# Gathering the rows of the first four expert blocks on chip, by matmuls with slot matrices

## The chip, the cores and the metric

The kernel runs on one core of one Trainium2 chip. The metric is device time of one execution in microseconds (us). A core has five engines that run their own instruction streams and meet at semaphores: TensorE (PE, matmuls and transposes into PSUM), VectorE (DVE), ScalarE (ACT), GpSimd (POOL, which here issues the indirect DMAs) and SyncE (SP, which here issues the plain DMAs). PEld is TensorE's loading of weights, which overlaps its matmuls.

## The reference

The kernel computes an audio tower for 64 samples of 10 tokens each (640 tokens of 128 features): a patch projection with a layer norm, one attention layer of 8 heads with a distance bias, and a mixture of 16 experts, of which each token uses the best two. The part that matters here is the last one:

```
router_logits = x @ router_w.T
top_vals, top_idx = jax.lax.top_k(router_logits, TOP_K)
weights = jax.nn.softmax(top_vals.astype(jnp.float32), axis=-1)
...
def step(acc, ew):
    wg, wu, wd, ce = ew
    hid = jax.nn.silu(x @ wg) * (x @ wu)
    y = hid @ wd
    return (acc + ce[:, None] * y, None)
```

The kernel computes an expert only for the tokens that chose it. All arithmetic is in float32.

## The kernel before

Tokens lie in five tiles t = 0..4 of 128 (one token per partition). After attention each tile goes through a chain of its own: PE projects it (`project(t)`), DVE and ACT normalise it into `pay[:, 0, t, 0:128]` (`normalised(t)`), PE transposes it (`normal_T(t)`) and multiplies it with the router (`logits(t)`), DVE takes the best two experts (`best(t)`, `route(t)`, which ends in `mask[:, t, :]`), PE counts with a triangular matrix how many tokens have gone to each expert so far (`ranks(t)`, `later_rows(t)`), and DVE reads out of these counts the slot of each token at each of its two experts (`place(t)`, which ends in `slot[:, t, :]`).

A slot is a row of `disp`, a buffer in memory of 16 x 640 rows; expert e owns the rows from 640 e on. A row has 131 numbers: 128 features and three that travel with them (where the result belongs, the weight, the token's number). POOL sends every tile twice, once for each choice: ten indirect DMAs (`dispatch(t, j)`, line 386). When all ten have landed (semaphore `s_disp`), SP loads the first 128 rows of experts 0, 1, 2, 3 into four buffers `xs` (line 327) and later, as buffers come free, those of the others (line 332).

An expert block e (there are 17: the 16 experts and one overflow block) then is: PE transposes its rows (`rows_T`, line 1082), ACT copies them to `xsT` and the three numbers to `meta` (`take_rows`, lines 556 and 557), PE multiplies with gate and up weights (`gate_up`, four matmuls, line 1087), ACT applies silu (line 562), DVE multiplies (`gated`, line 825), PE multiplies with the down weights (`down`, two matmuls, line 1095). A float32 matmul stands in the trace as two MATMUL instructions. PE runs its instructions in the written order: `rows_T(e+3)`, `gate_up(e+2)`, `down(e)`. For blocks 0 to 11 DVE scales the result (`result`, lines 831 and 832) and POOL sends it to `ybuf` in memory (line 395); SP fetches all of `ybuf` back (`yb`) once the twelve sends have landed. The last five blocks are added in PSUM by matmuls with 0/1 matrices that DVE makes (`spread`, `combine`, line 1103). Lines 877 to 883 add everything up on DVE.

Between the end of the routing and the first rows PE has nothing to do. The program fills part of this with matmuls of zeros (`keep_clock`, line 892), 24 of them from tile 3's ranks on, 16 of these behind the last `later_rows`.

When its counting is done, DVE runs a chain of small instructions that decide about overflow blocks (lines 797 to 819); the first `gated` stands behind it.

Of the kernel before, what the change touches and what calls it, by code (L numbers as in the profile page):

```python
# [10 lines left out]
ALU = mybir.AluOpType  # L11
# [3 lines left out]
P = 128  # L15
B = 64
S = 10
T = S // 2
D = 128
# [19 lines left out]
EARLY = 2  # L39

# [41 lines left out]
def audio_tower(nc, first, rows_d, gb, t_head, table, toks, expert_w, out):  # L82
    with ExitStack() as ctx:
# [78 lines left out]
        iota = sb("iota", [P, TOK])  # L162
        comb = sb("comb", [P, TAIL, TOK])
# [82 lines left out]
        comb_ready = sem("comb_ready")  # L246
        yt_ready = sem("yt_ready")
# [20 lines left out]
        GATE, ROWS_T, RESULT = (1, 3, 4, 0), 5, (7, 2)  # L268
        FIRST_ROWS = (5, 7, 2)
# [29 lines left out]
        OVER_ROWS = 4  # L299

        def combined(t):

            return ps[:, (6, 3)[t // 4], (t % 4) * D:(t % 4 + 1) * D]
# [4 lines left out]
        def _(sp):  # L308
# [17 lines left out]
            for u in range(NBUF):  # L326
                sp.dma_start(xs[:, u, :], disp[u * TOK:u * TOK + P, :]).then_inc(xs_in[u], 16)
            with sp.Fori(1, E // NBUF) as g:
                for u in range(NBUF):
                    row = sp.snap((g * NBUF + u) * TOK)  # L330
                    sp.wait_ge(xs_used, g * NBUF + (u - NBUF + 1))
                    sp.dma_start(xs[:, u, :], disp[bass.ds(row, P), :]).then_inc(xs_in[u], 16)
# [5 lines left out]
            sp.wait_ge(xs_used, E - NBUF + 1)  # L338
# [72 lines left out]
        def _(act):  # L411
# [141 lines left out]
            def take_rows(b, src, e, bank=ROWS_T):  # L553

                act.wait_ge(xsT_ps, e + 1)
# [8 lines left out]
            def take_result(b, n, e):  # L564

                act.wait_ge(y_ps, e + 1)
                nc.scalar.copy(yt[:, n, :], ps[:, RESULT[b], 0:D]).then_inc(yt_ready, 1)

            AHEAD = 3
            for e in range(AHEAD):  # L570
                take_rows(e, e, e, FIRST_ROWS[e])
            with act.Fori(0, E // NBUF - 1) as g:
                for u in range(NBUF):
                    silu(u, g * NBUF + u)
                    take_rows((u + AHEAD) % NBUF, (u + AHEAD) % NBUF, g * NBUF + (u + AHEAD))
            for e in range(E - NBUF, BLK):
# [18 lines left out]
        def _(dve):  # L595
# [150 lines left out]

            def place(t):
                dve.wait_ge(rank_ps, t + 1)
                need(mark(nc.vector.tensor_tensor(spick[:, t, :, :], oh[:, t, :, :],
                                                  count_ps().unsqueeze(1).broadcast_to([P, TOPK, E]), ALU.mult)))  # L750
                with nc.allow_low_precision(reason="one whole number below 2**24 among zeros"):
                    nc.vector.tensor_reduce(slot[:, t, :], spick[:, t, :, :], AX_X, ALU.add).then_inc(slot_ready, 1)

# [25 lines left out]
            route(1)  # L779
            stream_stats(3)  # L780
            place(1)
            best(2)
            normalised(3)
# [6 lines left out]
            place(3)  # L790
            best(4)
            route(4)
            place(4)

# [33 lines left out]
            def result(b, u, e):  # L828

                dve.wait_ge(y_ps, e + 1)  # L830
                nc.vector.tensor_copy(yi[:, u:u + 1], meta[:, bass.ds(e, 1), 0:1].rearrange("p a c -> p (a c)"))
                nc.vector.tensor_scalar(ys[:, u, :], ps[:, RESULT[b], 0:D],  # L832
                                        meta[:, bass.ds(e, 1), 1:2].rearrange("p a c -> p (a c)"), None,
                                        ALU.mult).then_inc(y_ready, 1)

            def spread(n, e):

                dve.wait_ge(xs_used, e + 1)
                dve.wait_ge(in_toks, 16)
                m = meta[:, bass.ds(e, 1), :].rearrange("p a c -> p (a c)")  # L840
                nc.vector.tensor_scalar(comb[:, n, :], iota[:, :], m[:, 2:3], m[:, 1:2],
                                        ALU.is_equal, ALU.mult).then_inc(comb_ready, 1)
# [12 lines left out]
            with dve.Fori(1, E // NBUF - 1) as g:  # L855
                for k in range(NBUF):
                    finish(k, g * NBUF + k)
                    gated((k + 2) % NBUF, g * NBUF + (k + 2))
            n_over = dve.value_load(ctl[0:1, 0:1], min_val=0, max_val=NOV)
            for e in range(E - NBUF, BLK):  # L860
# [25 lines left out]
        def _(pe):  # L886
# [176 lines left out]
            logits(3)  # L1063
            later_rows(2)
            keep_clock(2, FREED)
            ranks(3)
            normal_T(4)
            keep_clock(1, FREED)
            logits(4)
            later_rows(3)  # L1070
            keep_clock(3, FREED)
            ranks(4)
            keep_clock(2, FREED)
            later_rows(4).then_inc(cnt_ps, 1)
            keep_clock(16, FREED)
# [8 lines left out]
            def gate_up(b, e, w):  # L1084
                pe.wait_ge(xsT_ready, e + 1)
                for c in range(4):
                    last = mm(ps[:, GATE[b], c * P:(c + 1) * P],  # L1087
                              expW[:, w * WROW + c * P:w * WROW + (c + 1) * P], xsT[:, b, :], start=True, stop=True)
                last.then_inc(g_ps, 1)

            def down(b, r, e, w):
                pe.wait_ge(hid_ready, e + 2)
                for c in range(2):
                    a = w * WROW + 2 * F + c * D
                    last = mm(ps[:, RESULT[r], 0:D], hid[:, b, c, :], expW[:, a:a + D], start=(c == 0), stop=(c == 1))  # L1095
# [11 lines left out]
            def step(e):  # L1107

                if e + 3 < BLK:
                    n = (e + 3) % NBUF  # L1110
                    pe.wait_ge(xsT_ready, e + 3)
                    rows_T(n, e + 3, xs_in[n], 16 * ((e + 3) // NBUF + 1))
# [72 lines left out]
```

## Time and profile before

| | |
|---|---|
| time, median of 3 runs (lowest to highest) | 98.06 us (97.67 to 98.19) |
| profiled execution: its own time, its span | 97.58 us, 95.4 us |
| PE busy | 86.2 us, 90% of the span |
| DVE, ACT, POOL busy | 56.5 us (59%), 36.2 us (38%), 33.2 us (35%) |
| chain that ended last, by engine | PE 81%, DMA 4%, ACT 4%, issue 2%, DVE 2% |

The span runs from the first to the last instruction that the profiler recorded; 2.18 us of the profiled execution's time lie around it. The shares are averages over stages; what matters below is one stage, from about 47 us (the last tiles are routed) to about 63 us (the expert blocks run at their full pace). "Chain that ended last" follows the work back from the last instruction to what released it. PEclk is the clock that TensorE was granted, 1.00 being 2.4 GHz and 0.50 being 1.2 GHz.

### The profile page before, as it was taken

How to read it: one execution, taken by the hardware profiler on the slowest of the kernel's cores; microseconds unless marked ns; L12 is line 12 of the kernel's file. 1: busy time of each engine (PE TensorE's matmuls, PEld its weight loads, DVE VectorE, ACT ScalarE, POOL GpSimd, SP SyncE). 2: the span in 40 equal slices, each digit the busy share in tenths (PEclk: the TensorE clock that was granted, in tenths of full speed). 3: DMA queues.
4: the chain of work that ended last, by engine and by line, in shares of the span. 5: the costliest groups of instructions: out<-in, count | busy, mean ns of one | idle time of the engine just before them, and what ended most of it. 6: DMA issues, size and time to landing. Idle time of an engine off the chain costs nothing.

```text
span 95.4 us, 2194 instructions
## 1 busy us (share of the span) xinstructions
PE 86.2 (90%) x742; PEld 78.6 (82%) x742; DVE 56.5 (59%) x200; ACT 36.2 (38%) x138; POOL 33.2 (35%) x32
## 2 busy tenths in 40 slices
PE   5999997999999999999989946999999999999900
PEld 5996995776769699999868945999999999999800
DVE  2029878890789599895565820135566656696230
ACT  0402285504331233768678303243544534631000
POOL 6000006099960000046677700005766766400000
PEclk9999999999999999999999997599999999999995
DMA  2672999999999999941101114221322462153014
GB/s 28 251 290 101 413 419 420 386 393 271 340 412 414 422 448 419 343 124 56 56 28 56 56 41 107 56 56 49 81 77 59 95 165 82 37 131 150 0 28 110
DMA packets 7759, 17.83 MB, mean 187 GB/s; under 512 B 913, under 2 KB 5143, under 8 KB 7238
## 3 DMA queue, kind: packets, MB, share of 16 engines
q1 hardware_dynamic: 6420, 15.49, 46.0%
q0 software_dynamic: 704, 1.19, 3.7%
q10 hardware_dynamic: 626, 1.03, 3.0%
q8 instruction: 6, 0.10, 0.4%
q14 instruction: 3, 0.02, 0.1%
HBM read 10.17 MB, written 7.81 MB: 188 GB/s over the span
## 4 chain that ended last, share of the span: by engine, by line
PE 81%; DMA 4%; ACT 4%; issue 2%; DVE 2%; POOL 1%; SPq 0%; DVEq 0%; POOLq 0%; ACTq 0%
PE ps L1087 18%; PE ps L972 12%; PE ps L892 9%; PE ps L1095 8%; PE ps L955 7%; PE ps L1103 6%; PE ps L905 3%; PE ps L920 3%; DMA disp<-pay,slot 2%; PE ps L1082 2%; PE ps L985 2%; DMA xs<-disp 2%; PE ps L944 2%; PE ps L900 1%; PE ps L981 1%
## 5 line engine op out<-in xcount | busy, mean ns | idle before, releaser
L1087 PE MATMUL ps<-xsT,expW 128*128 128x128 f32 x136 | 19.5, 291 | 0.0
L1087 PEld LDWEIGHTS ps<-xsT,expW 128*128 128x128 f32 x136 | 18.0, 207 | 0.1
L395 POOL DMA_INDIRECT ybuf<-ys,yi x12 | 11.8, 984 | 15.8 <-DVE ys L832 10.5
L892 PE MATMUL ps<-zeros 128*128 128x128 f32 x112 | 15.5, 297 | 1.0 <-DVE zeros L607 1.0
L892 PEld LDWEIGHTS ps<-zeros 128*128 128x128 f32 x112 | 14.5, 209 | 1.6 <-DVE zeros L607 1.0
L386 POOL DMA_INDIRECT disp<-pay,slot x10 | 9.8, 976 | 17.0 <-ACT pay L502 13.8
L825 DVE TENSOR_TENSOR hid<-sg,ps 128x256 f32<-128x256 f32 x17 | 7.2, 421 | 11.6 <-ACT sg L562 11.2
L972 PE MATMUL ps<-cst,prodv 128*128 128x128 f32 x100 | 12.4, 280 | 0.0
L972 PEld LDWEIGHTS ps<-cst,prodv 128*128 128x128 f32 x100 | 11.6, 192 | 0.4 <-issue 0.4
L556 ACT COPY xsT<-ps 128x128 f32<-128x128 f32 x17 | 4.5, 265 | 17.9 <-PE ps L1082 17.9
L1095 PE MATMUL ps<-expW,hid 128*128 128x128 f32 x68 | 10.4, 275 | 0.0
L276 POOL TENSOR_TENSOR prod<-qT,kT 128x1280 f32<-128x1280 f32 x3 | 8.6, 2900 | 2.5 <-ACT qT L451 2.5
L1095 PEld LDWEIGHTS ps<-expW,hid 128*128 128x128 f32 x68 | 9.0, 192 | 0.0
L727 DVE TENSOR_TENSOR prodv<-v,ps 128x1280 f32<-128x1280 f32 x5 | 7.4, 1478 | 0.2
L955 PE MATMUL ps<-prod,cst 128*32 128x128 f32 (+1 forms) x100 | 7.4, 278 | 0.0
L562 ACT ACTIVATE sg<-ps 128x256 f32<-128x256 f32 x17 | 6.6, 386 | 0.9 <-PE ps L1087 0.6
L1082 PE MATMUL ps<-cst,xs 128*128 128x128 f32 x17 | 5.0, 292 | 2.1 <-DMA xs<-disp 2.0
L421 ACT ACTIVATE lnv<-mv,eps 128x1 f32<-128x1 f32 (+2 forms) x9 | 2.6, 293 | 9.8 <-DVEq L626 5.6
L371 POOL TENSOR_TENSOR hb<-h,gbo 128x640 f32<-128x640 f32 x1 | 1.5, 1532 | 13.1 <-DVE xn L650 13.1
L1103 PE MATMUL ps<-yt,comb 128*128 128x128 f32 x50 | 6.1, 276 | 0.0
L955 PEld LDWEIGHTS ps<-prod,cst 128*32 128x32 f32 (+1 forms) x100 | 4.7, 106 | 1.5 <-issue 1.0
L1103 PEld LDWEIGHTS ps<-yt,comb 128*128 128x128 f32 x50 | 5.8, 192 | 0.0
(127 smaller groups left out, 124.0 us busy)
## 6 DMA issues: line engine op xcount, KB each, us to landing
expW<-expert_w_dram SPq DMA_DIRECT2D x4, 1536.0 KB, 25.4
disp<-blank SPq DMA_DIRECT2D x1, 5240.0 KB, 18.0
xs<-disp SPq DMA_DIRECT2D x17, 65.5 KB, 1.9
cst<-table_dram ACTq DMA_DIRECT2D x1, 652.5 KB, 5.9
ybuf<-zeros SPq DMA_DIRECT2D x1, 640.0 KB, 29.0
xw<-first_dram SPq DMA_DIRECT2D x1, 480.0 KB, 3.5
expW<-expert_w_dram SPq DMA_DIRECT2D x1, 384.0 KB, 3.3
yb<-ybuf SPq DMA_DIRECT2D x1, 384.0 KB, 3.1
```

Of the source, the lines that this page charges most:

```text
L276: return engine.tensor_tensor(prod[:, i, a * P:b * P].rearrange("p (k r b) -> p k r b", k=b - a, r=2), q.rearrange("p (r b) -> p r b", r=2 ...
L386: nc.gpsimd.indirect_dma_start(out=disp, out_offset=bass.IndirectOffsetOnAxis(ap=slot[:, t, j:j + 1], axis=0), in_=pay[:, j, t, :], in_off ...
L395: nc.gpsimd.indirect_dma_start(out=ybuf, out_offset=bass.IndirectOffsetOnAxis(ap=yi[:, u:u + 1], axis=0), in_=ys[:, u, :], in_offset=None, ...
L727: nc.vector.tensor_tensor(prodv[:, i, :].rearrange("p (n d) -> p n d", d=DH), v[:, :].rearrange("p (n d) -> p n d", d=DH), weights_ps(i).u ...
L825: nc.vector.tensor_tensor(hid[:, b, :, :].rearrange("p c s -> p (c s)"), sg[:, b, :], ps[:, GATE[b], F:2 * F], ALU.mult).then_inc(hid_read ...
L892: mm(ps[:, bank, 0:P], zeros[:, :], zeros[:, :], start=True, stop=True)
L955: last = mm(ps[g:g + m, SCORES[i], P:2 * P], cst[:, w:w + m], prod[:, i, k * P:(k + 1) * P], start=False, stop=k in (3, 7, 9))
L972: last = mm(ps[:, HEADS, 0:P], prodv[:, i, k * D:(k + 1) * D], ident, start=(k == 0), stop=(k == S - 1))
L1082: nc.tensor.transpose(ps[:, bank, 0:P], xs[:, src, 0:D], ident).then_inc(xsT_ps, 1)
L1087: last = mm(ps[:, GATE[b], c * P:(c + 1) * P], expW[:, w * WROW + c * P:w * WROW + (c + 1) * P], xsT[:, b, :], start=True, stop=True)
L1095: last = mm(ps[:, RESULT[r], 0:D], hid[:, b, c, :], expW[:, a:a + D], start=(c == 0), stop=(c == 1))
L1103: last = mm(combined(t), comb[:, n, t * P:(t + 1) * P], yt[:, n, :], start=first and t % 4 == 0, stop=True, skip_group_check=True)
```

## The change

The rows of experts 0 to 3 (`NEAR = 4`) no longer come from `disp`. For every tile DVE makes a slot matrix: `near[p, e]` is the token's slot plus one if it chose expert e, else zero (one small instruction in `place`), and `match` compares it with the numbers 1 to 128 (plus 640 e) for each of the four experts. The result, 128 x 512 of zeros and ones, goes into `prod`, which attention no longer needs. PE multiplies each tile with its slot matrix and adds the tiles up in PSUM (`gather(t, half)`, two experts a half): this gives the rows of an expert already transposed. ACT copies each half into `xsT`. The sending of all rows to `disp` stays. SP loads the rows of experts 4 to 7 first, and with a DMA of its own, second in its queue, the three numbers that belong to the rows of experts 0 to 3.

```
@@ sync
+            sp.dma_start(iota[:, :], toks.partition_broadcast(P)).then_inc(in_toks, 16)
             for g in range(0, E, NBUF):
                 sp.dma_start(expW[:, g * WROW:(g + NBUF) * WROW],
                              expert_w[:, g * WROW:(g + NBUF) * WROW]).then_inc(in_expert, 16)
-            sp.dma_start(iota[:, :], toks.partition_broadcast(P)).then_inc(in_toks, 16)
...
             sp.wait_ge(s_disp, 16 * T * TOPK)
             for u in range(NBUF):
-                sp.dma_start(xs[:, u, :], disp[u * TOK:u * TOK + P, :]).then_inc(xs_in[u], 16)
+                row = (NEAR + u) * TOK
+                sp.dma_start(xs[:, u, :], disp[row:row + P, :]).then_inc(xs_in[u], 16)
+                if u == 0:
+                    sp.dma_start(meta[:, 0:NEAR, :],
+                                 disp[0:NEAR * TOK, :].rearrange("(e s) c -> s e c", s=TOK)[0:P, :, D:ROW]
+                                 ).then_inc(in_meta, 16)
@@ scalar, behind the loading of the silu table
+            for half in range(2):
+                act.wait_ge(near_ps, half + 1)
+                nc.scalar.copy(xsT[:, 2 * half:2 * half + 2, :].rearrange("p e s -> p (e s)"),
+                               ps[:, NEAR_ROWS[half], 0:2 * P]).then_inc(near_taken, 1)
+            for e in range(NEAR):
+                silu(e, e)
@@ vector, place(t) and match(t, a, b)
+                counted[t] = mark(nc.vector.scalar_tensor_tensor(near[:, t, :], count_ps()[:, 0:NEAR], 1.0,
+                                                                 mask[:, t, 0:NEAR], ALU.add, ALU.mult))
...
+                dve.wait_ge(in_toks, 16)
+                need(counted[t])
+                nc.vector.tensor_tensor(
+                    prod[:, t, a * P:b * P].rearrange("p (e s) -> p e s", s=P),
+                    iota[:, TOK + a * P:TOK + b * P].rearrange("p (e s) -> p e s", s=P),
+                    near[:, t, a:b].unsqueeze(2).broadcast_to([P, b - a, P]), ALU.is_equal).then_inc(near_ready, 1)
@@ vector, expert blocks
-            gated(0, 0)
-            gated(1, 1)
-            for e in range(2, 2 + NBUF):
-                finish(e - 2, e - 2)
+            for e in range(NEAR):
+                gated(e, e)
+            dve.wait_ge(in_meta, 16)
+            dve.wait_ge(y_ps, NEAR)
+            for e in range(NEAR):
+                result(e % 2, e, e)
+            for e in range(NEAR, NEAR + 2):
                 gated(e % NBUF, e)
@@ tensor
+            def gather(t, half):
...
+                pe.wait_ge(near_ready, t + 1 + (half if t == T - 1 else 0))
+                last = mm(ps[:, NEAR_ROWS[half], 0:2 * P], pay[:, 0, t, 0:D], near_rows(t, half),
+                          start=(t == 0), stop=(t == T - 1))
...
-            rows_T(0, 0, xs_in[0], 16, FIRST_ROWS[0])
-            rows_T(1, 1, xs_in[1], 16, FIRST_ROWS[1])
             gate_up(0, 0, 0)
-            rows_T(2, 2, xs_in[2], 16, FIRST_ROWS[2])
             gate_up(1, 1, 1)
-            for e in range(BLK):
+            gate_up(2, 2, 2)
+            down(0, 0, 0, 0)
+            gate_up(3, 3, 3)
+            down(1, 1, 1, 1)
+            down(2, 0, 2, 2)
+            rows_T(0, 4, xs_in[0], 16, FIRST_ROWS[0])
+            rows_T(1, 5, xs_in[1], 16, FIRST_ROWS[1])
+            down(3, 1, 3, 3)
+            pe.wait_ge(hid_ready, 2)
+            gate_up(0, 4, 4)
+            rows_T(2, 6, xs_in[2], 16, FIRST_ROWS[2])
+            pe.wait_ge(hid_ready, 3)
+            gate_up(1, 5, 5)
+            for e in range(NEAR, BLK):
```

The loops of ACT and DVE over the blocks are written out instead of looped, the temporary matrices `comb` now lie where `prodv` was, and some PSUM banks change places.

On PE, at the end of the routing and the start of the expert blocks, stood before (line 1005 is `ranks(4)`, 1013 `later_rows`, 892 the zeros, 1082 `rows_T`, 1087 `gate_up`, 1095 `down`):

```order
L1013 MATMUL ps<-mask,rest 128x16
L892 MATMUL ps<-zeros 128x128 x3
L1005 MATMUL ps<-mask,cst 128x16
L892 MATMUL ps<-zeros 128x128 x2
L1013 MATMUL ps<-mask,rest 128x16
L892 MATMUL ps<-zeros 128x128 x16
L1082 MATMUL ps<-cst,xs 128x128 x2
L1087 MATMUL ps<-xsT,expW 128x128 x4
L1082 MATMUL ps<-cst,xs 128x128
L1087 MATMUL ps<-xsT,expW 128x128 x4
```

At the same place on PE now stands (1055 `later_rows`, 1047 `ranks(4)`, 1112 `gather`, 1148 `gate_up`, 1156 `down`, 1140 `rows_T`):

```order
L1055 MATMUL ps<-mask,rest 128x16
L1112 MATMUL ps<-prod,pay 128x256 x2
L1047 MATMUL ps<-mask,cst 128x16
L1112 MATMUL ps<-prod,pay 128x256 x3
L1055 MATMUL ps<-mask,rest 128x16
L1112 MATMUL ps<-prod,pay 128x256 x2
L1148 MATMUL ps<-xsT,expW 128x128 x12
L1156 MATMUL ps<-expW,hid 128x128 x2
L1148 MATMUL ps<-xsT,expW 128x128 x4
L1156 MATMUL ps<-expW,hid 128x128 x4
L1140 MATMUL ps<-cst,xs 128x128 x2
L1156 MATMUL ps<-expW,hid 128x128 x2
```

The zeros are gone, gathers stand in their place, and the first transpose of loaded rows comes behind four `gate_up` and three `down`; `down(3)` stands behind the transposes of blocks 4 and 5.

On DVE, from `ranks(4)`'s mask to the chain about overflow blocks, now stands (768 is the mask of tile 4, 774, 776 and 780 are `place(4)`, 786 is `match`, 840 the first of the chain):

```order
L768 TENSOR_TENSOR mask<-oh 128x16
L786 TENSOR_TENSOR prod<-iota,near 128x512
L774 TENSOR_TENSOR spick<-oh,ps 128x32
L776 SCALAR_TENSOR_TENSOR near<-ps,mask 128x4
L780 TENSOR_REDUCE slot<-spick 128x2
L786 TENSOR_TENSOR prod<-iota,near 128x256 x2
L840 TENSOR_TENSOR chosen<-ps,cst 1x16
```

Before, the mask, two instructions of `place(4)` and the chain followed each other directly; added are the `match` of tile 3 ahead of `place(4)`, one small instruction in it, and the `match` of tile 4 in two halves behind it.

## Rows read from the trace of the kernel before

**Rows 1.** Chain that ended last, in order of time: start us, us, what.

```profile
53.72 2.32 DMA disp<-pay,slot
...
56.43 1.96 DMA xs<-disp
...
58.43 0.42 PE ps L1082
...
62.48 0.89 PE ps L1087 x8
63.38 0.45 PE ps L1095 x4
63.82 0.11 PE ps L1082
...
87.13 3.36 PE ps L1103 x30
```

**Rows 2.** Timeline of PE from 52 us: start, us, line, in brackets idle time before.

```profile
52.22 3.82 PE L892 MATMUL ps<-zeros 128*128 128x128 f32 x32
57.99 0.86 PE L1082 MATMUL ps<-cst,xs 128*128 128x128 f32 x2 [1.96 <-DMA xs<-disp]
```

**Rows 3.** Windows: us, busy PE, PEld, DVE, ACT, POOL, then PEclk, DMA share, GB/s.

```profile
58.43:62.37 3.94, 3.94 (x20) 3.86 (x21) 0.42 (x1) 1.26 (x7) 0.00 (x0) 0.57 0.23 57
62.37:82.66 20.29, 20.29 (x185) 20.29 (x184) 11.63 (x39) 9.74 (x44) 11.81 (x12) 1.00 0.30 81
```

**Rows 4.** Timeline of DVE, end of the routing: mask of tile 4, first and last of the chain.

```profile
50.85 0.17 DVE L745 TENSOR_TENSOR mask<-oh 128x16 f32<-128x16 f32 x1
...
52.41 0.16 DVE L797 TENSOR_TENSOR chosen<-ps,cst 1x16 f32<-1x16 f32 x1 [0.49 <-PE ps L1013]
...
55.36 0.16 DVE L819 CAST ctl<-eor 1x9 int32<-1x9 f32 x1
```

**Rows 5.** Groups by form: line, engine, shape, count | busy us, mean ns | idle.

```profile
L877 DVE TENSOR_TENSOR acc<-h,yb 128x256 f32<-128x256 f32 x1 | 0.4, 419 | 0.0
L444 ACT COPY xnT<-ps 128x256 f32<-128x256 f32 x3 | 0.9, 381 | 0.8 <-PE ps L916 0.8
```

**Rows 6.** Timeline of ACT behind the routing.

```profile
53.21 0.20 ACT L551 ACTIVATE actw<-ones 1x1 f32<-1x1 f32 x1
```

**Rows 7.** Timeline of SP's queue: start, us, DMA issues.

```profile
56.05 1.76 SPq L327 DMA_DIRECT2D xs<-disp  x4
...
91.43 0.58 SPq L358 DMA_DIRECT2D out_dram<-acc  x1
```

**Rows 8.** DMA issues of the whole page: KB each, median us to landing.

```profile
xs<-disp SPq DMA_DIRECT2D x17, 65.5 KB, 1.9
...
out_dram<-acc SPq DMA_DIRECT2D x1, 160.0 KB, 2.8
```

**Rows 9.** DMA queue 1 from 56 to 60 us: packets, MB, share of 16 engines.

```profile
q1 hardware_dynamic: 621, 0.29, 32.4%
```

**Rows 10.** The same from 13 to 42 us.

```profile
q1 hardware_dynamic: 2663, 10.93, 98.7%
```

**Rows 11.** Timeline of POOL: a dispatch, and three of the twelve sends of results.

```profile
49.93 0.95 POOL L386 DMA_INDIRECT disp<-pay,slot  x1 [0.30 <-issue]
...
75.51 0.98 POOL L395 DMA_INDIRECT ybuf<-ys,yi  x1 [0.47 <-issue]
76.91 0.98 POOL L395 DMA_INDIRECT ybuf<-ys,yi  x1 [0.41 <-issue]
...
81.31 0.98 POOL L395 DMA_INDIRECT ybuf<-ys,yi  x1 [0.47 <-issue]
```

**Rows 12.** Timeline of DVE: a comparison during that dispatch, and the sums at the end.

```profile
50.63 0.19 DVE L742 TENSOR_TENSOR oh<-cst,topi 128x32 f32<-128x32 f32 x1
...
88.32 0.42 DVE L878 TENSOR_TENSOR acc<-acc,yb 128x256 f32<-128x256 f32 x1
90.52 0.69 DVE L881 TENSOR_TENSOR acc<-acc,ps 128x512 f32<-128x512 f32 x1 [1.77 <-PE ps L1103]
```

More of the change, by code:

```diff
@@ L39 @@
 EARLY = 2
+NEAR = 4
 C_ID = 0
@@ L161, in audio_tower @@
         yb = sb("yb", [P, T, TOPK, D])
-        iota = sb("iota", [P, TOK])
-        comb = sb("comb", [P, TAIL, TOK])
+        iota = sb("iota", [P, TOK + NEAR * P])
+        near = sb("near", [P, T, NEAR])
+        comb = prodv
         yt = sb("yt", [P, TAIL, D])
@@ L297, in stream_ps, with result_ps, near_rows @@
             return ps[:, SCORES[t], 3 * P:3 * P + D]
-        OVER_ROWS = 4
+        OVER_ROWS = 1
+        def result_ps(b, e):
+            first = P if isinstance(e, int) and e in (2, 3) else 0
+            return ps[:, RESULT[b], first:first + D]
+        def near_rows(t, half):
+            return prod[:, t, half * 2 * P:(half + 1) * 2 * P]
         def combined(t):
-            return ps[:, (6, 3)[t // 4], (t % 4) * D:(t % 4 + 1) * D]
+            return ps[:, (6, 4)[t // 4], (t % 4) * D:(t % 4 + 1) * D]
         block = ctx.enter_context(nc.Block())
@@ L566, in take_result @@
                 act.wait_ge(y_ps, e + 1)
-                nc.scalar.copy(yt[:, n, :], ps[:, RESULT[b], 0:D]).then_inc(yt_ready, 1)
-            AHEAD = 3
[L570 to L576, printed above, removed]
+                nc.scalar.copy(yt[:, n, :], result_ps(b, e)).then_inc(yt_ready, 1)
+            for half in range(2):
[4 more added lines that the diff above has]
+                silu(e, e)
+            AHEAD = 3
+            for e in range(NEAR, NEAR + AHEAD):
+                take_rows(e % NBUF, e % NBUF, e, FIRST_ROWS[e - NEAR])
+            for e in range(NEAR, BLK):
                 silu(e % NBUF, e)
@@ L779, in _ @@
             route(1)
+            match(0, 0, NEAR)
             stream_stats(3)
@@ L782, in _ @@
             best(2)
+            match(1, 0, NEAR)
             normalised(3)
@@ L790, in _ @@
             place(3)
+            match(2, 0, NEAR)
             best(4)
             route(4)
+            match(3, 0, NEAR)
             place(4)
+            match(4, 0, 2)
+            match(4, 2, NEAR)
             dve.wait_ge(cnt_ps, 1)
@@ L848, in finish @@
                 result(n % 2, n, e)
-            gated(0, 0)
-            gated(1, 1)
-            for e in range(2, 2 + NBUF):
-                finish(e - 2, e - 2)
+            for e in range(NEAR):
[5 more added lines that the diff above has]
+            for e in range(NEAR, NEAR + 2):
                 gated(e % NBUF, e)
[L855 to L858, printed above, removed]
             n_over = dve.value_load(ctl[0:1, 0:1], min_val=0, max_val=NOV)
-            for e in range(E - NBUF, BLK):
+            for e in range(NEAR, BLK):
                 if e < SENT_Y:
@@ L1063, in _ @@
             logits(3)
+            def gather(t, half):
+                if t == 0 and half == 0:
+                    pe.wait_ge(h2_ready, 2)
+                    pe.wait_ge(x2_ready, 2)
+                pe.wait_ge(near_ready, t + 1 + (half if t == T - 1 else 0))
+                last = mm(ps[:, NEAR_ROWS[half], 0:2 * P], pay[:, 0, t, 0:D], near_rows(t, half),
+                          start=(t == 0), stop=(t == T - 1))
+                if t == T - 1:
+                    last.then_inc(near_ps, 1)
             later_rows(2)
-            keep_clock(2, FREED)
+            gather(0, 0)
+            gather(0, 1)
             ranks(3)
             normal_T(4)
-            keep_clock(1, FREED)
+            gather(1, 0)
             logits(4)
             later_rows(3)
-            keep_clock(3, FREED)
+            gather(1, 1)
+            gather(2, 0)
             ranks(4)
-            keep_clock(2, FREED)
+            gather(2, 1)
+            gather(3, 0)
+            gather(3, 1)
             later_rows(4).then_inc(cnt_ps, 1)
-            keep_clock(16, FREED)
+            gather(4, 0)
+            gather(4, 1)
             pe.wait_ge(h2_ready, T)
```

44 lines of the change are left out of this document (28 added, 16 removed).

## Prediction

> **What bounds the kernel now.** I read the chain that ended last first. PE holds 81% of it, so the kernel is mostly a row of matmuls, and the question is where PE stands idle or slow. The chain in order of time shows one such place [rows 1]: the last dispatch starts at 53.72 us and takes 2.32 to land, the load of the rows 1.96 more, and the first transposes of rows come at 58. PE's timeline shows what it does meanwhile [rows 2]: matmuls of zeros until 56.04, then 1.96 us of nothing. The windows show what follows [rows 3]: from 58.43 to 62.37 the granted clock is 0.57 on average, so PE falls to its lower level after the idle stretch, and from 62.37 on it is 1.00. So this stage costs twice: the wait for memory, and slow matmuls behind it. From there on PE is busy all the time (20.29 of 20.29 us) until 87.13 + 3.36 = 90.49 [rows 1], and 4.9 us of tail follow (95.4 - 90.49).
>
> **Prices of a block, at full clock.** One transpose 0.11, `gate_up` 0.89 (eight MATMUL rows), `down` 0.45, one `combine` 3.36/3 = 1.12 [rows 1]. From 58.43 to 90.49, 32.06 us, PE does 16 transposes, 17 `gate_up`, 17 `down` and 5 `combine`: 1.76 + 15.13 + 7.65 + 5.60 = 30.14. The missing 1.92 us is the slow clock.
>
> **When the gathered rows are ready.** In the last tiles DVE has gaps, and the `match` of tiles 0 to 2 falls into them or ahead of work that waits for PE anyway. What counts is the end. Price of a `match`: no row has a comparison of 128x512; a sum of two operands of 128x256 took 0.42 and one of 128x512 (an operand in PSUM) 0.69 [rows 5, 12], so I take 0.69 alone and 0.6 in a row of instructions that overlap. The bounds are 0.42 and, if the broadcast operand halved the pace, 1.4. The mask of tile 4 ends at 51.02 [rows 4]; `match(3)` runs to 51.6 and pushes `place(4)` by 0.1; the halves of `match(4)` are ready at about 52.35 and 52.7. The small instruction in `place` falls into the wait between its two neighbours: nothing.
>
> On PE a gather has 256 columns against 128 in one matmul of `gate_up` (0.89/4 = 0.22), so 0.45 each, ten of them 4.5 us. They take the place of 24 matmuls of zeros (24 x 0.22 = 5.3 us), so up to `ranks(4)` nothing moves. After `ranks(4)` (51.3) stand five gathers and `later_rows`: 51.3 + 5 x 0.45 + 0.15 = 53.7. ACT ends its preparation of silu at 53.41 [rows 6] and copies a half in 0.38 [rows 5], so `gate_up(0)` starts at about 53.75. The chain about overflow blocks starts with `later_rows`, at 52.85 instead of 52.41, lasts 3.11 as before (to 55.52) and ends at 55.96; behind it stand the first `gated`, 0.42 each. `down(0)` stands behind three `gate_up`, at 53.75 + 2.67 = 56.42, when `gated(0)` has just ended (56.4): no wait, but no room. Four `gate_up` and three `down` end at 53.75 + 3.56 + 1.35 = 58.7.
>
> **When the next rows land.** The dispatches are not touched: POOL sends one every 1.25 us to the end (0.95 and 0.30 between [rows 11]), so SP still issues at 56.05 [rows 7]. Block 4's rows land at 58.0 as before [rows 2], and PE doesn't wait for them. But block 5's, which `rows_T` of block 5 needs with all of PE's later work queued behind it, are now third in SP's queue, behind the load of the three numbers: 4 x 128 pieces of 12 bytes. Issuing: 128 pieces took 1.76/4 = 0.44, 320 pieces 0.58 [rows 7], so 192 pieces more cost 0.14 and 512 come to 0.72. Block 5 is issued at 56.43 + 0.8 = 57.2 and lands 1.9 to 1.96 later [rows 1, 8]: 59.2 at best. It stands behind the 512 pieces in the same queue. A row of 524 bytes took 0.324 x 16 x 4 us / 621 = 33 ns of an engine [rows 9], so 32 pieces for each of the 16 engines take 1.1 us, most of which passes while block 5 is issued. The output, 320 pieces of 512 bytes, landed 2.8 after its issue [rows 8], with a second one as large beside it; by that the three numbers land near 58.9 and block 5 at 59.4. I take X = 59.4. The lower bound is 59.2. No row has pieces of 12 bytes; the dearest packets of the trace, 4 KB ones with every engine full, took 0.987 x 16 x 29 us / 2663 = 172 ns [rows 10], and with those the pieces alone take 5.5 us: issued at 56.43, flowing from 57.4, block 5 would land near 64. The stage is quiet and the pieces are small, so the 33 ns row is the nearer one.
>
> The Trainium skill speaks against this DMA: "DMA: Bandwidth & Descriptors", section "Specifications", asks for at least 512 B in a piece, below which the engine reads, modifies and writes. It gives no price; if each piece cost twice the 33 ns, an estimate, X would be 60.5. The trace of before cannot show it.
>
> **The sum.** From X on PE has 12 transposes, 13 `gate_up`, 14 `down` (that of block 3 stands behind) and 5 `combine`: 1.32 + 11.57 + 6.30 + 5.60 = 24.8 us, against 32.06 from 58.43 before. The gain is 32.06 - 24.8 - (X - 58.43) = 7.3 - (X - 58.43). With X = 59.4 that is 6.3. In parts: 4.9 us of blocks done while memory was waited for, 0.4 of transposes that are gone, 1.9 of clock, less 1.0 because block 5 lands later than block 1 did. PE ends at 84.2. The wait at block 5 is 59.4 - 58.8 = 0.6 us, too short, I think, to lose the clock (1.96 lost it). It also covers the routing: `match` or the chain may be 0.6 late at no cost, beyond that each us costs one.
>
> Two more queues. ACT stands `silu(4)` behind the three copies of rows 4 to 6 and DVE stands `gated(4)` behind the wait for the three numbers and eight small instructions for blocks 0 to 3; PE needs `gated(4)` only at X + 3.4, after two `gate_up`, a transpose and `down(3)`, so both have a us to spare. And POOL's sends start later: the first results come at X + 1.1 = 60.5 instead of 64.3, four at once. The twelve sends took as little as 1.40 apart (75.51 to 76.91), always waiting for a result [rows 11]; at that pace from 61.4 the last starts at 76.8. Before, the sums of the fetched results ended at 88.74, 7.4 after the last send started [rows 11, 12]. So they end at 84.2, just when PE does: no cost, 0.5 us at a pace of 1.45. The longer load of `iota` ahead of the weights moves bulk traffic that ends near 42 us [rows 10]; the weights are needed at 53.75.
>
> So 97.58 - 6.3 = 91.3 by the profiled execution's own time. The median of the runs stands 0.5 above it; I put the time at 91.5.
>
> **Rivals.** (1) *The small pieces jam the queue*, X at 61 or later, and PE idles 2 us again, as long as the idle time that cost the clock before. The gain is 7.3 - 2.6 = 4.7, or 2.8 if the 1.9 of slow clock comes back: 92.9 to 94.8. For it: no row shows such pieces. Against: 33 ns in this very stretch.
>
> (2) *`match` and the dispatches hold each other up*, so that `s_disp` comes later. Three `match` fall into the last dispatches. A comparison with both operands in SBUF took its usual 0.19 inside a dispatch of 0.95, and neither was longer than elsewhere [rows 11, 12]; but it is short. If each of the last three (0.6 + 0.6 + 0.6 in two halves) stopped POOL, X would be 61.2 and the gain 4.5, or 2.6 with the clock lost: 93.1 to 95.0. The Trainium skill has such a rule in "SBUF — State Buffer", section "Who interferes with whom": a VectorE instruction with two SBUF inputs contends with a GpSimd instruction that reads SBUF. The rows above don't show it.
>
> (3) *Slower than before*, by one mechanism: the pieces of 12 bytes cost so much that the work done early is lost again. With the slow clock behind the wait this takes X above 58.43 + 7.3 - 1.9 = 63.8. The pieces flow from 57.4 and block 5 needs 1.2 more, so 5.2 us for 32 pieces, 163 ns each, is the point where it decides; at 200 ns it would be 98.8. Only the packets of the saturated stage cost that much.
>
> (4) *It does not do what it says*: block 5 gates PE in any case, so the wait only moves. That holds for the wait; but four blocks are behind PE by then, 4.9 us that no later wait takes back. No chance of its own beyond (3).
>
> **Chances.** My forecast, X from 59.2 to 60.0: 91.05 on the profiled base, less 0.35 for the spread of runs, to 92.3 on the median's, so 90.7 to 92.3: 0.66. (1) 0.22. (2) 0.07. (3) 0.05. The range 90.7 to 94.6 holds the first and most of the next two, about 0.8. Faster by over 0.5% (about what three runs from 97.67 to 98.19 can tell apart): 0.94; within it, from the edge of (3): 0.02; slower: 0.04.
>
> **What would show it.** The profile after should have `gate_up(0)` at 53.5 to 54, clock 1.00 from there to the end of the matmuls, one wait of PE near 58.8 put down to the load of `xs`, of 0.4 to 1.2 us, and the end of the last `combine` near 84. The dispatches should keep 0.95 and their steps of 1.25. If `match` takes over 0.8, or the load of the three numbers over 3 us, or the clock falls behind that wait, the forecast fails on that term.

## The result, and the profile after

The changed kernel ran in 93.88 and 93.04 us, the kernel before beside it in 97.67 to 98.19: a ratio of 0.954, with a 95% interval of 0.942 to 0.966. It is faster, as forecast, and the time lies in the range of 90.7 to 94.6, but above the 90.7 to 92.3 of the forecast proper, 1.5 to 2.4 us above the 91.5 that I gave. Some executions of every kernel, before as well, take 2 to 10 us longer, where profiled mostly because the first stage does, and they are left out of all times and ratios, which leaves `after_again`, `waits48` and `waits24` one time each; the profiles of `after_again`, `shift72`, `before_filled`, `waits48` and `waits24` come from such executions, so theirs are read from the last dispatch on.

The profiled execution took 93.88 us, its span is 91.7. Of the page, the busy times, and the shares of the chain that ended last:

```profile
PE 83.6 (91%) x710; PEld 74.9 (82%) x710; DVE 58.7 (64%) x211; ACT 35.8 (39%) x132; POOL 34.0 (37%) x32
...
PE 72%; DMA 11%; SPq 4%; issue 3%; ACT 3%; DVE 2%; POOL 2%; DVEq 0%; POOLq 0%; ACTq 0%
```

PE is busy 2.6 us less than before, but DMA holds 11% of the chain instead of 4%. In order of time (start us, us, what) the chain has this at the end of the routing and towards its end:

```profile
53.32 0.96 POOL disp L407
...
54.59 4.10 DMA disp<-pay,slot
...
58.70 0.33 SPq L344
...
59.55 1.99 DMA xs<-disp
...
61.59 0.33 PE ps L1140
...
73.95 3.65 DMA xs<-disp
...
77.74 0.30 PE ps L1140
...
83.91 3.37 PE ps L1164 x30
```

Against [rows 1] the last dispatch starts 0.87 us later and takes 4.10 to land where it took 2.32. That is the surprise: nothing in the change touches how a dispatch lands. SP's first load of rows is issued at 58.70 instead of the predicted 56.05. PE's timeline (start, us, line, in brackets idle time before) shows what this costs:

```profile
54.63 2.92 PE L1148 MATMUL ps<-xsT,expW 128*128 128x128 f32 x24
...
60.53 0.33 PE L1140 MATMUL ps<-cst,xs 128*128 128x128 f32 x1 [0.69 <-DMA xs<-disp]
61.59 0.33 PE L1140 MATMUL ps<-cst,xs 128*128 128x128 f32 x1 [0.73 <-DMA xs<-disp]
...
77.74 0.30 PE L1140 MATMUL ps<-cst,xs 128*128 128x128 f32 x1 [0.44 <-DMA xs<-disp]
```

The four blocks that were gathered on chip run from 54.63 on. Then PE waits twice, 0.69 and 0.73 us, and once more at the last block. The windows (busy PE, PEld, DVE, ACT, POOL, PEclk, DMA share, GB/s) show that the clock holds behind the waits, where it was 0.57 before [rows 3]:

```profile
60.00:62.00 2.00, 0.74 (x5) 0.56 (x6) 0.00 (x0) 0.41 (x3) 0.00 (x0) 1.00 0.57 106
62.00:64.00 2.00, 2.00 (x21) 2.00 (x20) 1.46 (x8) 0.91 (x5) 0.26 (x1) 1.00 0.29 72
```

Where did the last dispatch lose 1.8 us? The DMA queues (packets, MB, share of 16 engines) in four stretches, 56.0 to 56.3, 56.3 to 56.6, 57.4 to 57.8 and 57.8 to 58.7; between them, from 56.6 to 57.4, no packet starts:

```profile
q0 software_dynamic: 15, 0.06, 61.8%
...
q8 instruction: 1, 0.02, 22.8%
q0 software_dynamic: 15, 0.00, 2.2%
...
q0 software_dynamic: 1, 0.00, 7.3%
...
q0 software_dynamic: 1, 0.00, 0.2%
```

Queue 0 carries the dispatch. Fifteen of its sixteen data packets are on their way by 56.3, and their fifteen tiny ones, which report the end, by 56.6. Just then queue 8 starts one packet that takes 0.228 x 16 x 0.3 = 1.09 us of one engine. The sixteenth data packet comes only behind it, at 57.6, and its report in the last stretch. Queue 8 holds six packets and 0.10 MB in the whole execution: it fetches PE's program, in blocks of 16 KB (below, it moves when PE's instructions do). The Trainium skill, "Runtime: NRT & Kernel Launch", section "Instruction fetch mechanics", says that an engine's program is refilled in blocks of 16 KiB, 256 instructions each, by a DMA queue that its sequencer drives, and calls the cost of crossing a block "mostly hidden". The size and the queue of their own agree with this trace (how many instructions are in a block, no run here shows); the cost was not hidden here: the block stood in front of the last packet that everybody waited for. In the kernel before the fetch nearest to this place came at 58.9 us, when the dispatch had landed.

A second thing differs. POOL's dispatches (start, us), four of the ten:

```profile
43.69 1.46 POOL L407 DMA_INDIRECT disp<-pay,slot  x1 [0.31 <-issue]
45.45 1.11 POOL L407 DMA_INDIRECT disp<-pay,slot  x1 [0.30 <-ACT pay L508]
...
51.92 1.10 POOL L407 DMA_INDIRECT disp<-pay,slot  x1 [0.30 <-issue]
53.32 0.96 POOL L407 DMA_INDIRECT disp<-pay,slot  x1 [0.30 <-issue]
```

And the `match` comparisons of DVE:

```profile
43.63 0.69 DVE L786 TENSOR_TENSOR prod<-iota,near 128x512 f32<-128x512 f32 x1
...
45.06 0.67 DVE L786 TENSOR_TENSOR prod<-iota,near 128x512 f32<-128x512 f32 x1
...
51.50 0.69 DVE L786 TENSOR_TENSOR prod<-iota,near 128x512 f32<-128x512 f32 x1
...
52.46 0.76 DVE L786 TENSOR_TENSOR prod<-iota,near 128x256 f32<-128x256 f32 x2
```

Apart from the first, which takes 1.14 in both kernels, three dispatches are longer than the usual 0.95 [rows 11], and they are the three that start while a 128x512 comparison runs. The longer the rest of the comparison, the longer the dispatch: 1.46 with 0.63 us to go, 1.11 and 1.10 with 0.28 and 0.27. The comparisons keep their 0.67 to 0.69. This is the mechanism of rival (2), at a small price: the last dispatch is 54.59 - 53.72 = 0.87 late, of which 0.55 lie in the first stage (the first dispatch starts at 42.24, before at 41.69) and 0.32 here. That the change costs the 0.55 is not shown: the first dispatch starts at 41.69 to 42.14 in three profiles without the change (below, `before48` and `before_waits`) and at 41.81 to 42.24 in five with it.

### The profile page after: what moved, and what is told of

Read it like the earlier page. It is cut to its first block, busy times and chain, and to the rows that moved or that the text cites. A ratio compares the mean times of both kernels' runs of the same rounds, so it can differ in the third digit from the quotient of the medians.

```text
span 91.7 us, 2056 instructions
## 1 busy us (share of the span) xinstructions
PE 83.6 (91%) x710; PEld 74.9 (82%) x710; DVE 58.7 (64%) x211; ACT 35.8 (39%) x132; POOL 34.0 (37%) x32
## 4 chain that ended last, share of the span: by engine, by line
PE 72%; DMA 11%; SPq 4%; issue 3%; ACT 3%; DVE 2%; POOL 2%; DVEq 0%; POOLq 0%; ACTq 0%
PE ps L1014 13%; PE ps L934 10%; PE ps L1148 8%; PE ps L997 7%; DMA xs<-disp 6%; PE ps L1164 6%; DMA disp<-pay,slot 4%; PE ps L1156 4%; PE ps L947 3%; PE ps L962 3%; PE ps L1027 2%; PE ps L986 2%; POOL disp L407 2%; PE ps L942 2%; PE ps L1140 1%
## 5 line engine op out<-in xcount | busy, mean ns | idle before, releaser
L1148 PE MATMUL ps<-xsT,expW 128*128 128x128 f32 x136 | 17.7, 276 | 0.1
L1148 PEld LDWEIGHTS ps<-xsT,expW 128*128 128x128 f32 x136 | 16.4, 192 | 0.5 <-issue 0.5
L407 POOL DMA_INDIRECT disp<-pay,slot x10 | 10.6, 1056 | 16.5 <-ACT pay L523 14.1
L934 PE MATMUL ps<-zeros 128*128 128x128 f32 x64 | 9.4, 316 | 1.0 <-DVE zeros L630 1.0
L934 PEld LDWEIGHTS ps<-zeros 128*128 128x128 f32 x64 | 8.9, 226 | 1.6 <-DVE zeros L630 1.0
L577 ACT COPY xsT<-ps 128x128 f32<-128x128 f32 x13 | 3.4, 265 | 11.6 <-PE ps L1140 11.6
L1164 PE MATMUL ps<-yt,prodv 128*128 128x128 f32 x50 | 6.1, 275 | 0.0
L1164 PEld LDWEIGHTS ps<-yt,prodv 128*128 128x128 f32 x50 | 5.8, 192 | 0.0
L1112 PE MATMUL ps<-prod,pay 128*128 128x256 f32 x20 | 5.4, 396 | 0.0
```

Source lines behind the costliest of these rows:

```text
L407: nc.gpsimd.indirect_dma_start(out=disp, out_offset=bass.IndirectOffsetOnAxis(ap=slot[:, t, j:j + 1], axis=0), in_=pay[:, j, t, :], in_off ...
L934: mm(ps[:, bank, 0:P], zeros[:, :], zeros[:, :], start=True, stop=True)
L1148: last = mm(ps[:, GATE[b], c * P:(c + 1) * P], expW[:, w * WROW + c * P:w * WROW + (c + 1) * P], xsT[:, b, :], start=True, stop=True)
L1164: last = mm(combined(t), comb[:, n, t * P:(t + 1) * P], yt[:, n, :], start=first and t % 4 == 0, stop=True, skip_group_check=True)
```

## The experiments

Each was run beside the kernel before on one chip, and its ratio is against that; the chip is not the same for all experiments. Theory A: the 16 KB fetch of PE's program, by the place where it falls, delays the last dispatch. Theory B: the 4.10 us were chance. Theory C: the comparisons hold POOL's dispatches back, and by that the landing.

**`after_again`: the changed kernel, unaltered.**

> The changed kernel, unaltered. Theory A (a 16 KB fetch of PE's own instructions, which sits on one DMA engine for 1.1 us just when the last dispatch's data arrive, holds back that engine's sixteenth): the last dispatch takes about 4 us from its start to the first issue of SP behind it, again, with the instruction packet between 56 and 57 us. Theory B (chance in the memory's answer): this time 2.3 us, as before the change, in most profiles. Time: A 93 to 94, B about 92.

It took 92.42 us, below the 93 to 94 that I expected of theory A and nearer to the 92 of theory B, so the time doesn't decide. The landing does. From the profile's chain, and its DMA queues from 63.36 to 63.6 and from 64.9 to 65.2:

```profile
61.63 4.44 DMA disp<-pay,slot
...
q8 instruction: 1, 0.02, 41.6%
...
q0 software_dynamic: 1, 0.00, 9.7%
```

The last dispatch takes long again, with a fetch at 63.4 that takes 1.6 us of an engine and the sixteenth data packet behind it, and PE waits 1.09 and 1.02 for blocks 4 and 5, with the clock kept. So it isn't chance.

**`shift72` and `shift48`: fewer and wider zeros at the start.** The 24 zeros matmuls of the input stage become 6 of four times, or 12 of twice the width: the same columns, 72 or 48 instructions fewer, so that every later fetch moves.

```
+            def keep_wide(n, wide, bank=IDLE):
+                for _ in range(n):
+                    mm(ps[:, bank, 0:wide * P].rearrange("p (w c) -> p w c", w=wide), zeros[:, :],
+                       zeros[:, :].unsqueeze(1).broadcast_to([P, wide, P]), start=True, stop=True)
...
-            keep_clock(24)
+            keep_wide(12, 2)
```

> The 24 filler matmuls of zeros at the start become 6 of four times the width: same PE time, 72 PE instructions (4.6 KB) fewer, so every later fetch of PE's program comes 72 instructions later. Theory A: the fetch that fell at 56.5 comes behind the loads of the blocks' rows; the last dispatch takes 2.3 us, SP issues at 56.9 to 57.1, block 5 lands near 59.9, the load of block 16's rows takes 2.3 instead of 3.6; time 1.5 to 2.5 us below the changed kernel's. Theory B, and a third one, C (the comparisons on DVE hold up POOL and so the landing): no difference beyond 0.5 us.

> The same with 12 fillers of double width, 48 PE instructions fewer. Theory A: the fetch falls 48 instructions later, among the loads of rows and of the three numbers near 59 us; the last dispatch takes 2.3 us, but one of those loads (block 5's or 6's, or the three numbers) lands up to 1.1 us late; time between that of the changed kernel and of the 72-instruction one. Theories B and C: as the changed kernel.

`shift48` took 91.67, 91.73 and 91.74 us (ratio 0.934, 0.927 to 0.941). Its chain that ended last:

```profile
54.56 2.27 DMA disp<-pay,slot
...
57.70 2.31 DMA xs<-disp
...
81.68 3.36 PE ps L1170 x30
```

The last dispatch starts as in the changed kernel and lands in 2.27; the fetches lie at 62.1 and 75.8 and delay nothing. That I expected it to hit the loads of rows was wrong: they had landed. `shift72` took 91.75 and 92.25 (0.937, 0.928 to 0.947). There the last dispatch lands in 2.26, but the fetch, at 66.0, meets the first sending of a result; its chain:

```profile
64.50 3.77 DMA ybuf<-ys,yi
...
68.37 0.34 DVE ys L875
68.71 0.34 DVE hid L868
...
69.09 0.71 PE ps L1162 x4
```

DVE waits 2.04 us for the buffer that this send empties, and PE loses 0.4 us (two `gate_up` there start 1.89 apart, the others 1.45). The victim changes, the mechanism doesn't.

**`before48`: the kernel before with the zeros of `shift48`.**

> The kernel before with the same 12 double-width start-up zeros as shift48 and nothing else. If the wider zeros by themselves gained anything, it would be under 97.4; by the theory of the fetch they change only when PE's instructions are fetched, and the kernel before shows no transfer delayed by a fetch at its critical place (last dispatch 2.32), so 97.6 to 98.4, ratio 0.995 to 1.005. If a fetch now hits one of its small transfers, up to 2 us slower, and the trace shows which.

Seven runs from 97.44 to 98.74, ratio 0.997 (0.992 to 1.001). Wider zeros alone gain nothing that these runs can tell from zero.

```
-            keep_wide(12, 2)
+            for _ in range(12):
+                keep_wide(1, 2)
+                for _ in range(8):
+                    pe.wait_ge(zeros_set, 1)
```

> The changed kernel with the start-up zeros as in shift48 (12 of double width instead of 24), and 12 zeros matmuls of 4 columns more behind them: PE's instruction count is that of the changed kernel again, its start-up work nearly that of shift48. If the fetch of PE's instructions is what delays the last packet of the last dispatch, it comes near 56.5 us again, the last dispatch takes about 4 us to land, and the time is 94.0 to 94.8. If something about the wider start-up matmuls themselves made shift48 fast (their load on PE, the clock), the last dispatch lands in 2.3 and the time is 91.7 again.

> shift48 with eight waits on a semaphore that is long set behind each of the 12 double-width start-up zeros: 48 instructions more for PE, its program as long as the changed kernel's again, and, so I expect, no work and no time of PE more (the zeros matmul ahead of them covers them), which was the fault of refill48. Theory of the fetch: it is back at about 56.5 us, the last dispatch takes about 4.1 us to land instead of 2.3, PE waits 1.2 to 1.6 us for blocks 4 and 5, and the time is 93.0 to 94.5. Rival (the doubled matmuls themselves, or chance, made shift48 fast): 2.3 us to land and 91.5 to 91.9.

> The same with four waits behind each: 24 instructions more than shift48, 24 fewer than the changed kernel. By the theory of the fetch it lies between 56.5 (changed kernel) and 62.1 (shift48), so at about 58 to 60, when the loads of the rows and of the three numbers are on their way: the last dispatch lands in 2.3, and one of the loads of blocks 4 to 7 takes up to 1.1 us longer than the 1.9 to 2.3 of shift48. If it is block 4's or 5's, PE waits 0.5 to 1.3 us and the time is 92.0 to 92.8; if block 6's or 7's, 91.5 to 91.9. Rival: no load is delayed by the fetch, rows in flight or not.

`refill48` was a poor control: 98.42 and 99.27 us. A zeros matmul of 4 columns costs as much as one of 128 (2.58 us for twelve), and the first dispatch came 4.0 us later than in `shift48`; the other 1.4 lie around 19 to 22 us, where the granted clock is 0.50, in `shift48` 1.00. But the collision was back (4.08 us to land, PE waits of 0.61 and 1.31), and here the clock fell: two of its windows,

```profile
67.00:68.00 1.00, 1.00 (x7) 1.00 (x6) 0.97 (x6) 0.00 (x0) 0.00 (x0) 0.50 0.02 6
68.00:69.00 1.00, 1.00 (x7) 1.00 (x6) 0.43 (x3) 0.19 (x2) 0.77 (x1) 0.50 0.25 69
```

show 0.50, the lower level, and two `gate_up` took 1.71 and 1.58 instead of 0.89, which is 1.5 us more. 91.7 + 4.0 + 1.8 + 1.5 = 99.0. `waits48` is the clean one: the zeros take the same 5.45 us in both profiles, only PE's program is as long as the changed kernel's again. It took 93.19 us. Its chain:

```profile
57.79 4.04 DMA disp<-pay,slot
...
62.70 2.33 DMA xs<-disp
```

And two rows of PE's timeline:

```profile
63.63 0.33 PE L1149 MATMUL ps<-cst,xs 128*128 128x128 f32 x1 [0.59 <-DMA xs<-disp]
65.08 0.33 PE L1149 MATMUL ps<-cst,xs 128*128 128x128 f32 x1 [1.12 <-DMA xs<-disp]
```

The fetch is at 59.6, 1.8 us into the dispatch as in the changed kernel (1.9). With `waits24` it comes 24 instructions later, and there the loads of rows are in flight; its chain:

```profile
61.59 2.33 DMA disp<-pay,slot
...
64.79 3.10 DMA xs<-disp
```

And its DMA issues from 63.9 to 68 (KB each, median us to landing):

```profile
xs<-disp SPq DMA_DIRECT2D x5, 65.5 KB, 2.5
meta<-disp SPq DMA_DIRECT2D x1, 6.0 KB, 3.4
```

Block 5's rows take 3.10 us instead of 2.31, the three numbers 3.4 instead of 2.1, and PE waits 0.99; it took 92.17 us, inside what was expected. `waits48`, `waits24` and `shift48` differ in instructions without work, and they took 93.19, 92.17 and 91.7 us. These differences are rough, since the changed kernel's own times go from 92.42 to 93.88; that what the fetch meets decides is shown by the waits of PE.

One more reading supports theory A. In all four profiles in which the last dispatch lands late (the changed kernel, `after_again`, `refill48`, `waits48`) its sixteenth data packet starts 1.2 to 1.7 us behind the fifteenth and within 0.02 us of the fetch's end, as at 57.58 and 57.60 in the changed kernel. In the ten other profiles no fetch runs beside these packets, and all sixteen start within 0.17 us of each other.

**`before_waits`: can the fetch hurt the kernel before?** 24 instructions more by the same waits, two behind each zeros matmul of the input stage.

> The kernel before with two waits on a semaphore that is long set behind each of the 24 start-up zeros, which makes PE's program 24 instructions longer and adds no work: does the fetch hurt any kernel whose last dispatch it meets? In the profile of before it came at 58.9 us, behind some 15 instructions of PE from the end of its wait; 24 instructions earlier is near 55.5, while the last dispatch (53.72 to 56.04) is landing. Theory of the fetch: the last dispatch takes 3.5 to 4.4 us instead of 2.3, PE waits 3 to 4 us instead of 2, and the time is 99 to 100.3 (98.1 and 1.0 to 2.1 more; the clock behind the wait is lost in both). Rival: 97.7 to 98.5, as before48. Other fetches move too; should one of them now spare the kernel a stall, the trace shows it.

It did not: 97.58 to 98.32 us, ratio 0.999 (0.996 to 1.002), the last dispatch 2.42 to land. I had aimed wrong: the fetch came at 53.4, before the last dispatch started at 54.11. It met an earlier one, started at 51.57; the DMA issues from 51.5 to 52:

```profile
disp<-pay,slot POOLq DMA_INDIRECT x1, 3.4
```

It took 3.4 us to land where the kernel before takes 2.3, and the next one took 3.0, but both landed ahead of the last. So the fetch delays dispatches of the kernel before too, and costs nothing where nobody waits for them. That the kernel before would pay if its last dispatch were met is not shown. In `before48` a fetch at 79.6 met the last load of rows, which took 3.56 us, and PE waited 0.45 for it, as in the changed kernel at 77.74.

**`before_filled`: the clock term by itself.** The kernel before with 9 of its last 16 zeros of double width, so that PE is busy until the rows are there.

```
-            keep_clock(16, FREED)
+            keep_clock(7, FREED)
+            keep_wide(9, 2, FREED)
```

> The kernel before the change, with 9 of the 16 last filler matmuls twice as wide, so that PE is busy until 57.9 instead of 56.0 (as many instructions as before). If the term of 1.92 us for the slow clock is right, the granted clock stays 1.00 behind the wait and the time falls by 1.5 to 1.9 us, to about 96.3. If the first blocks are slow for another reason, no change; if the fillers end too late, slower by up to 0.3.

96.06 to 96.79 us, ratio 0.982 (0.974 to 0.990): 1.8 us gained without any work done earlier. In its profile the rows come at 67.84, and a window behind that reads

```profile
69.00:70.00 1.00, 1.00 (x11) 1.00 (x10) 0.00 (x0) 0.23 (x2) 0.00 (x0) 1.00 0.19 42
```

so the first `gate_up` run at full pace. By the interval the gain is 1.0 to 2.6 us, which fits the 1.92 of the prediction.

**`meta_last48` and `meta_last48b`: the load of the three numbers last.** `shift48` with that DMA behind all four loads of rows.

```
-                if u == 0:
+                if u == NBUF - 1:
                     sp.dma_start(meta[:, 0:NEAR, :],
```

> shift48 with the load of the three numbers issued behind the four loads of rows instead of behind the first. Prediction's price: block 5's load was put 1.0 us late by this DMA (0.72 to 0.8 of issuing, the rest by its 512 pieces ahead in the queue). Measured in shift48: issuing took 0.43 and block 5's rows landed 2.31 after their issue, against 1.9 to 2.0 elsewhere. So I expect block 5 issued 0.45 earlier and landed about 0.8 earlier (59.2 instead of 60.0), PE's wait at block 5 (0.2 to 0.4 us) gone, and a time 0.3 to 0.4 below shift48 (91.3 to 91.5), unless the three numbers, now last, arrive behind the first result that needs them. Rival: pieces of 12 bytes cost nothing but their issue, then block 5 lands 0.45 earlier, with the same end on PE within 0.1.

> The same kernel as meta_last48, measured again, since its runs were spread from 90.72 to 98.41 there: is it faster than shift48's 91.7 where nothing disturbs it? Expected 90.7 to 91.2, 0.5 below shift48, which is PE's wait at block 5 (0.2 to 0.4 us) and the load of block 5 no longer behind 512 small pieces. If runs near 94.5 are as many again, a transfer of it is delayed in half of its executions, and the profile of one should show the fetch beside it.

The first took 90.72 and 91.17 us, the second 91.05, 91.37 and 91.56 (ratio 0.9355, 0.930 to 0.941). SP's queue in the second:

```profile
56.42 1.76 SPq L344 DMA_DIRECT2D xs<-disp  x4
58.23 0.43 SPq L346 DMA_DIRECT2D meta<-disp  x1
```

And the first transposes of loaded rows on PE, with no wait ahead of them:

```profile
59.23 0.38 PE L1146 MATMUL ps<-cst,xs 128*128 128x128 f32 x2
```

PE's wait at block 5, 0.4 us in `shift48`, is gone. The first measurement lies below the 91.3 to 91.5 that I expected, the second mostly above its 90.7 to 91.2. All five times are 0.1 to 1.0 us below `shift48`'s 91.7, but on other chips, and the two ratios, 0.9355 and 0.934, don't separate the two programs: that this one is faster is not shown. DVE now waits a us for the three numbers (1.01 in the first), but PE never for DVE.

**`dbl48`: twice the comparison.** `shift48` with the comparison of tile 3 made a second time into an unused part of `prod`.

```
             match(3, 0, NEAR)
+            match_again(3)
```

> shift48 with the comparison of tile 3 made twice (the second result goes into an unused part of prod, 0.68 us of DVE). Theory (lock): a dispatch that starts while a comparison runs begins only when it has ended. The comparisons of tile 4 move 0.68 later, to about 53.1 to 53.9, so the dispatch that starts at 53.30 is held by up to 0.6 and the last dispatch with it: the semaphore of all dispatches 0.5 to 0.6 later than in shift48 (57.4 instead of 56.85), and the second copy itself (52.2 to 52.9) lengthens the dispatch at 51.89 by up to 0.7 more if a comparison that follows at once takes the port again. Rival (no lock, the longer dispatches were chance): dispatches as in shift48, semaphore at 56.85. In both the gathers of tile 4 and the chain about overflow blocks are 0.68 later; PE's wait at block 5 covers 0.2 to 0.4 of it. Time 92.0 to 92.8 with the lock, 91.9 to 92.2 without.

91.35, 91.56 and 91.99 us (0.933, 0.924 to 0.942): nothing lost. DVE at the place:

```profile
51.24 0.69 DVE L786 TENSOR_TENSOR prod<-iota,near 128x512 f32<-128x512 f32 x1
51.84 0.68 DVE L794 TENSOR_TENSOR prod<-iota,near 128x512 f32<-128x512 f32 x1
...
52.80 0.78 DVE L786 TENSOR_TENSOR prod<-iota,near 128x256 f32<-128x256 f32 x2
```

And POOL:

```profile
51.67 1.08 POOL L407 DMA_INDIRECT disp<-pay,slot  x1 [0.30 <-ACT pay L520]
53.12 0.96 POOL L407 DMA_INDIRECT disp<-pay,slot  x1 [0.36 <-DVE slot L780]
```

The dispatch at 51.67 waits out the comparison that is running and not the one behind it; the dispatch at 53.12 falls into the two halves and keeps its 0.96. So my expectation of 0.6 us more failed: here a dispatch lost no more than the rest of one comparison. The 0.6 us of DVE were also hidden, because PE's row of gathers was behind anyway: it reached `gate_up(0)` at 54.53, 12.54 us after the first dispatch started, and in `shift48` at 54.61, 12.38 after it.

## Why the prediction was right, and where it was off

**Right: the mechanism and its parts.** Four blocks run during the wait, their transposes are gone, and the clock holds. `match` took 0.69, as taken from the rows, and its halves 0.76 together; the gathers ran in the row as planned; `gate_up(0)` came at 54.63, behind the 53.5 to 54 that I had named: it is 53.75 plus the 0.55 us of the first stage and 0.33 that I have not followed up. In `shift48` block 5's rows land at 57.70 + 2.31 = 60.01 and PE ends at 81.68 + 3.36 = 85.04: 25.0 us, predicted 24.8. The waits of 0.69 and 0.73 kept the clock, as did 0.59 and 1.12 in `waits48`; 1.96 [rows 2] and the 1.31 of `refill48`, behind 0.61, lost it.

**Wrong: "so SP still issues at 56.05".** It issues at 58.70. Of the 2.65 us, 0.55 are the first stage, 0.32 the comparisons, and 1.78 the fetch in front of the last dispatch's last packet. The step said that the dispatches are not touched. But the landing time of a dispatch was taken as a constant, 2.32, and the change moved PE's instructions, and by them the moment of the fetch, from 58.9 to 56.5. I had counted the DMAs that the program issues, not those that an engine issues for itself. Without the collision the same work takes 91.7 us (`shift48`), 0.2 from the forecast, in part by errors that cancel: PE ends 0.8 later there than predicted, and the tail is 0.4 shorter.

That the range still held is luck. Its part above 92.3 stood for rivals (1) and (2), and neither made this time. The number alone would have fitted rival (2), whose three halts were to cost 1.8 us; the landing and the shifted programs tell the two apart.

**The small pieces: about right in sum, wrong in parts.** The load of the three numbers was to issue for 0.72 to 0.8; it took 0.43, landing 2.1 after. From 58.7 to 62 the queue moved 1081 packets in 41.1% of 16 engines, 20 ns each; its 512 pieces of 12 bytes took 8.7 ns of an engine each, a quarter of the 33 of a row. Block 5 landed 61.54 - 58.70 = 2.84 us behind SP's first issue, where I had put 59.4 - 56.05 = 3.35. But this profile is the exception: with the loads in the same order and no fetch beside them it is 3.15 to 3.36 in six others (`after_again`, `shift72`, `shift48`, `refill48`, `waits48`, `dbl48`), because block 5's own load takes 2.29 to 2.50 and not 1.9 to 1.96. With the small load last it is 2.53 and 2.31 (`meta_last48`, `meta_last48b`). So the small load makes block 5 0.3 to 1.0 us late, and the 1.0 of the sum was near the upper end. Rival (1), a jam that takes block 5 to 61 or later by the pieces, and with it rival (3) fall. The Trainium skill asks for at least 512 B in a piece in "DMA: Bandwidth & Descriptors", section "Specifications". The doubled 33 ns that I had tried as its price do not show in these pieces.

**Rival (2)** is real and small. The Trainium skill, "SBUF — State Buffer", section "Who interferes with whom", is borne out: POOL waits for a comparison with two operands in SBUF, 0.32 us over the ten dispatches, not the 1.8 that I would have had to add. My counter-evidence, a comparison of 0.19 inside a dispatch, proved nothing, since it did not run when the dispatch started.

**The sum.** PE ends at 83.91 + 3.37 = 87.28, predicted 84.2. Block 5's first transpose starts at 61.59, 2.19 later than X: 2.65 - 0.51 + 0.05, where 0.51 is 3.35 - 2.84. The remaining 0.89 lie behind it, 0.44 of them the wait at the last block, whose load took 3.65 us beside the fetch at 75.4. The tail is 4.4 instead of 4.9, which I have not followed up. So 91.7 instead of 89.1 by the span. That POOL's sends cost nothing was right: they go 1.29 apart, and the last sum waits 1.93 for PE, not PE for it.

## What to carry to other kernels

When a change moves an engine's instructions, it can move that engine's program fetches too, as here on PE. Look at them in the queues of the profile: where one fell on a small transfer that all engines waited for, it cost 0.7 to 2.2 us (92.42 to 93.88 against 91.7), and 48 instructions more or fewer at a harmless place decided it. Before judging a restructuring by its time, shift the program by some instructions without work; a difference of the two times that only this makes is not the restructuring's.

Work put into the idle time of an engine pays twice where the clock would have fallen. In the kernel before, longer matmuls of zeros alone gained 1.8 us by keeping the clock, without any work done earlier.

## What the hardware showed that I had not expected

- One 16 KB fetch of PE's program holds one DMA engine for 1.1 us (1.6 in `after_again`), and a last dispatch of 16 data packets that meets it lands in 4.04 to 4.44 us instead of 2.26 to 2.42.
- An indirect DMA of POOL that starts during a comparison of DVE with two SBUF operands waits for the rest of it (0.95 becomes 1.08 to 1.46), but not for the next comparison.
- 512 pieces of 12 bytes were issued in 0.43 us and landed in 2.1, near the 1.9 of a load of 128 rows. Each took 8.7 ns of a DMA engine, a row of 524 bytes 33.
- A zeros matmul of 4 columns took 0.215 us, as long as one of 128.
